# A two-layer decoder on one core: Gram products moved into the LoRA feed-forward, weights of the last stage loaded in one go, and a new row order in the first attention

## The reference

```
x = x + gqa(ln(x))            # 16 query heads, 4 key heads of 128, layer norm of q and k, rotation, causal
x = x + cross0(ln(x), ctx)    # 8 heads of 8 rows, no weights
x = x + lora_ffn(ln(x))       # W_base x + b, and one of 8 rank-16 experts chosen by a router
x = x + mqa(ln(x))            # 16 heads of 16, one key head
x = x + cross1(ln(x), ctx)    # 16 heads of 128, rms norm of q and k over all 2,048 columns
x = x + quantised_ffn(ln(x))  # int8-like rounding of rows and weights
```

## Time and profile before

| what | value |
|---|---|
| median of 3 runs | 3075.42 us (3070.69 to 3077.81) |
| profiled execution, its own time | 3078.19 us |
| span in the profile, first to last instruction | 3076.4 us |
| mean granted TensorE clock | 0.958 of full speed |
| busy: PE / DVE / ACT / POOL | 86 / 66 / 51 / 46% |

### The profile page before, as it was taken

The page is one execution under the profiler, slowest core; times in us unless marked ns, Lnnn a source line. Parts: engine busy times, 40 slices in busy tenths (PEclk is TensorE's granted clock), DMA queues, the critical chain, the costliest instruction groups (busy, mean ns, idle before and its releaser), DMA issues. The chain is left out here.

```text
span 3076.4 us, 86672 instructions
## 1 busy us (share of the span) xinstructions
PE 2646.2 (86%) x33275; PEld 1934.0 (63%) x33291; DVE 2017.7 (66%) x3674; ACT 1573.7 (51%) x2950; POOL 1405.2 (46%) x1522
## 2 busy tenths in 40 slices
PE   3888888888876888886779989999999999999576
PEld 2677777777751222222468867888888888888333
DVE  5888888888866788884878862343434343433697
ACT  3565555556544677772134433444444444444587
POOL 4888888888852223322434421222222222222487
PEclk9999999999996899997989989999999999999899
DMA  3000000000002232320011110000000000000000
GB/s 125 2 0 0 0 0 0 0 0 0 0 1 86 83 94 86 91 82 11 0 39 31 34 52 31 7 4 4 5 3 5 3 5 3 5 32 1 4 24 27
DMA packets 94668, 75.60 MB, mean 25 GB/s; under 512 B 17520, under 2 KB 88560, under 8 KB 93424
## 3 DMA queue, kind: packets, MB, share of 16 engines
q1 hardware_dynamic: 94576, 74.35, 7.9%
HBM read 55.97 MB, written 17.04 MB: 24 GB/s over the span
## 5 line engine op out<-in xcount | busy, mean ns | idle before, releaser
L1394 DVE TENSOR_REDUCE x_mx<-x_ps 128x2 f16<-128x512 f32 x512 | 332.8, 683 | 57.2 <-PE x_ps L1458 54.3
L1363 ACT ACTIVATE x_e<-x_ps 128x512 f32<-128x512 f32 x512 | 292.2, 596 | 55.1 <-PE x_ps L1462 38.1
L361 POOL TENSOR_TENSOR x1s<-x1s,x1mx 128x1024 f32<-128x1024 f32 x32 | 60.8, 1900 | 519.0 <-DVE x1mx L357 519.0
L1458 PE MATMUL x_ps<-x_k,x_q 32*128 32x256 f16 x1024 | 199.4, 292 | 80.9 <-ACT x_e L1363 48.0
L1722 ACT ACTIVATE x_q<-x_ps,x_q_bias,x_q_scale 128x128 f32<-128x128 f32 x512 | 185.7, 467 | 159.7 <-PE x_ps L105 159.7
L1458 PEld LDWEIGHTS x_ps<-x_k,x_q 32*128 32x128 f16 x1024 | 58.1, 93 | 269.4 <-DVE x_mx L1394 130.4
L431 ACT CAST x1oh<-x_ps 128x1024 f16<-128x1024 f32 x64 | 64.7, 1012 | 313.0 <-PE x_ps L423 313.0
L103 PE MATMUL a_ps<-ln_xha,a_wq 128*128 128x128 f16 x1024 | 180.3, 222 | 51.2 <-ACT a0v L678 44.0
L627 POOL TENSOR_TENSOR a_w<-a_qsw,a_tab 128x512 f32<-128x512 f32 x128 | 176.6, 1380 | 57.3 <-ACT a_qsw L688 56.0
L1462 PE MATMUL x_ps<-x_q,x_k 32*128 32x256 f16 x1024 | 201.0, 293 | 1.7 <-ACT x_e L1363 1.4
L280 DVE TENSOR_TENSOR ln_xlx<-x_ps,ln_xhx 128x256 f16<-128x256 f32 x32 | 13.6, 424 | 281.6 <-ACT x_xt L1714 281.6
(11 more groups left out here) (369 smaller groups left out, 9144.1 us busy)
## 6 DMA issues: line engine op xcount, KB each, us to landing
x_q<-x_q_rows SPq DMA_DIRECT2D x32, 256.0 KB, 2.8
x_k<-x_k_rows SPq DMA_DIRECT2D x32, 256.0 KB, 3.1
a_stage<-in_x_w SPq DMA_DIRECT2D x32, 256.0 KB, 2.6
x_vt<-in_ctx_v SPq DMA_DIRECT2D x32, 144.0 KB, 2.3
stage<-in_x_wt SPq DMA_DIRECT2D x4, 1028.0 KB, 6.4
x_all<-in_x SPq DMA_DIRECT2D x8, 512.0 KB, 10.0
x_cf<-in_ctx SPq DMA_DIRECT2D x32, 128.0 KB, 2.1
x_q_rows<-x_xhl SPq DMA_DIRECT2D x32, 128.0 KB, 1.7
```

The costliest lines, as they stand in the source:

```text
L1363: act.activation(e[:, u % ES].rearrange("p c n -> p (c n)"), s2_ps(u), ACT.Exp, scale=XT ** -0.5).then_inc(e_ready, 1)
L1394: dve.reduce_max(mx[:, p % 2, c:c + 2], s1_ps(u), AX).then_inc(mx_ready, 1)
L1458: return pe.matmul(s1_ps(u)[:, c], q[r, p % 4, g, c * P:(c + 1) * P], k[r, p % 4, g], start=True, stop=True)
```

## The change

1. The 32 weight products leave the head of `attention_cross`. `ffn_lora` makes one of them in every tile, between the projections of t+1 and `transpose_h` of t. Its weights arrive one head at a time (129 KB) into four buffers `wt`, loaded by SyncE. Both results of a half (16 heads) share bank 7, which a matmul with a zero operand opens; after tile 16 and after the last tile ScalarE and VectorE split them (`gram_high`, `gram_low`) into `gh`, `gl`, `g2`, which now live in tensors around both functions. `ht_ps` moves from bank 7 to the unused columns of the banks of `a_ps`. The new helper `over_halves` unrolls four tiles at the start, eight in the middle and four at the end.
2. In `attention_cross` SyncE loads the quantised ffn's weights right behind the first two context tiles, since `stage` has no other use.
3. In `attention_gqa` the order changes on three engines: TensorE makes the bias scores first in a step. VectorE takes `vq` ahead of the raw keys, sums the raw keys only before the maximum, takes query group 0 behind the denominator, normalisation and the low part of the output ahead of it, and the next rows' low part ahead of query group 3 and of the residual. ScalarE makes the swapped copy of group 0 before its squares, and the second high part of the output before the exponential. A query rotation now also waits for the squares.

```diff
+def over_halves(eng, head, step):
+    mid = TILES // 2
+    head()
+    for t in range(4):
+        step(t, t, True, 0)
...
 # attention_gqa, scalar: the copies are split off from square()
+            def swap_query(t, g):
+                act.wait_ge(q_ready, 4 * t + g + 1)
...
                 if has_next:
+                    swap_query(t + 1, 0)
                     square(t + 1, 0)
-                if has_next:
                     square(t + 1, 1)
-                at_.exponential(act, t)
-                if has_next:
-                    value(t + 1, 1 - p)
+                    swap_query(t + 1, 1)
                 if before:
                     at_.high(act, t - 1, 1, not has_next)
+                at_.exponential(act, t)
+                if has_next:
+                    value(t + 1, 1 - p)
 # attention_gqa, vector
-                if has_next:
-                    keys_raw(t + 1, 1 - p)
                 dve.wait_ge(var_ready, t + 1)
                 dve.tensor_scalar(vq[:, :], var_ps, ...)
                 if has_next:
-                    keys_summed(t + 1, 1 - p)
+                    keys_raw(t + 1, 1 - p)
+                    keys_summed(t + 1)
...
+                if has_next:
+                    keys_joined(t + 1, 1 - p)
                 at_.take_max(dve)
                 if has_next:
-                    rotate_query(t + 1, 0)
                     keys_scaled(t + 1, 1 - p)
                     rotate_query(t + 1, 1)
-                    add_swapped(t + 1, 0)
-                at_.denominator(dve, ch, t)
+                if further(t):
+                    ln.normalise(dve, t + 2, p)
                 if before:
                     at_.low(dve, t - 1, 1, not has_next)
-                if further(t):
-                    ln.normalise(dve, t + 2, p)
-                if has_next:
+                at_.denominator(dve, ch, t)
+                if has_next:
+                    rotate_query(t + 1, 0)
+                    add_swapped(t + 1, 0)
                     rotate_query(t + 1, 2)
                     add_swapped(t + 1, 1)
+                if further(t):
+                    ln.low(dve, t + 2, p)
+                if has_next:
                     rotate_query(t + 1, 3)
                 if before:
                     at_.add(dve, t - 1)
-                if further(t):
-                    ln.low(dve, t + 2, p)
 # attention_gqa, tensor
+                bias_scores(t, p)
                 if has_next:
                     keys(t + 1, 1 - p)
...
                 query_sums(t)
-                bias_scores(t, p)
 # ffn_lora, sync
+            def step(t, p, has_next):
+                wait_used(sp, wt_used, t, 4)
+                sp.dma_start(wt[:, p, :], dram_tile(d["x1_wt"], t)).then_inc(wt_in[p], 16)
+            over_tiles(sp, lambda: None, step, 4)
 # ffn_lora, scalar, after tile 16 and after the last
+            def gram_high(j):
+                act.wait_ge(wt_used, TILES // 2 * (j + 1))
+                for i, (src, twice) in enumerate(blocks):
+                    last = act.activation(gh[:, j, i], src, ACT.Copy, scale=twice * GRAM_SCALE)
+                last.then_inc(gh_ready, 1)
 # ffn_lora, vector, after tile 16 and after the last
+            def gram_low(j):
+                dve.wait_ge(gh_ready, j + 1)
+                for i, (src, twice) in enumerate(blocks):
+                    dve.scalar_tensor_tensor(gl[:, j, i], src, twice * GRAM_SCALE, gh[:, j, i], ALU.mult, ALU.subtract)
+                ...
 # ffn_lora, tensor
+            def weight_product(h, slot, start=False, stop=False):
+                pe.wait_ge(wt_in[slot], (h - slot) * 4 + 16)
+                w = wt[:, slot, :]
+                if start:
+                    pe.matmul(ps[:, 7, 0:GRAM + P + 1], zero[:, 0:P], zero[:, :], start=True, stop=False)
+                pe.matmul(g_high, w[:, 0:P], w, start=False, stop=False)
+                pe.matmul(g_low, w[:, P:2 * P], w[:, P:GRAM], start=False, stop=stop).then_inc(wt_used, 1)
...
+                if half == 0:
+                    weight_product(t, p, static and t == 0, static and t == TILES // 2 - 1)
+                elif static and t == TILES // 2 + 1:
+                    pe.wait_ge(gl_ready, 1)
+                    weight_product(t - 1, 0, True, False)
+                elif not (static and t == TILES // 2):
+                    weight_product(t - 1, (p - 1) % 4)
                 transpose_h(t, p)
...
 # attention_cross, sync
-            n = 2 * HEADS // GRAM_PIECES * GRAM
-            for i in range(GRAM_PIECES):
...
+            sp.dma_start(stage[:, 0:F1_COLS], d["f1_gu"]).then_inc(f1_in, 16)
+            sp.dma_start(stage[:, F1_COLS:], d["f1_down"]).then_inc(f1_in, 16)
...
-            sp.wait_ge(wt_used, GRAM_PIECES)
-            sp.dma_start(stage[:, 0:F1_COLS], d["f1_gu"]).then_inc(f1_in, 16)
-            sp.dma_start(stage[:, F1_COLS:], d["f1_down"]).then_inc(f1_in, 16)
 # attention_cross, scalar, vector and tensor heads: the splits, weight_products() and its wait go
-                weight_products()
-                pe.wait_ge(gl_ready, 2)
                 gram(0, 0)
```

148 lines of the change are left out of this document (78 added, 70 removed).

## The result

| | median us | runs | ratio to before, 95% interval |
|---|---|---|---|
| before | 3074.76 | 3070.69 to 3077.81, 4 | 1 |
| changed kernel | 3040.3 | 3037.72 to 3062.84, 4 | 0.9899 [0.9855, 0.9943] |
| changed kernel, timed again | 3049.14 | 3040.48 to 3054.78, 4 | 0.9921 [0.9894, 0.9948] |

A forecast was written before the change was run, and what follows sets the result against it. It took VectorE's chain to close the gqa step and TensorE alone to fill cross1's head; -37 (gqa), -23 (head) and +6 (LoRA ffn) gave -54, so 3021 us, own range 3003 to 3034, stated range 2985 to 3050.

The forecast's parts named there:

- 3039: Rival in gqa: the raw keys' sum waits for GpSimd's whole instruction (1.84 us), step gains only 0.60; chance 0.09.
- 3041: Rival in the LoRA ffn: the moved product is paid in full, +26 us there; chance 0.09.
- 3049: Rival in gqa: GpSimd closes the cycle, its late low squares leaving only 0.3 us gain a step; chance 0.14.
- From the keys to the scaled scores: Gqa step on VectorE: without the raw keys' sum, the scaled scores start right behind GpSimd's power, -0.49 us.
- From there to the low part of the rows: Gqa step on VectorE: denominator wait gone -0.57, low part earlier -1.38, raw keys' sum added +1.25 us.
- TensorE and GpSimd keep up: Gqa step: VectorE stays last with 1.0 us to spare; GpSimd's last low squares are the tight place.
- TensorE's bound: Rival in gqa: fewer port meetings, step shrinks by 2.2 us to what TensorE allows, 2990 us; chance 0.17.
- Gqa in all: Gqa stage: 31 steps, each 1.19 us shorter, -37 us, with ends of -55 and -31.
- Cross1's head: Start of the second cross attention: 32 weight products and their splits go, -23 us.
- The LoRA ffn: LoRA ffn: the product fits into TensorE's wait for routed rows; +6 us together, ends +3 and +26.
- Cross1's body: Second cross attention from 1862 us on: full of TensorE and not touched, so no term.
- The weights' loads at once: Quantised ffn's weights arriving at cross1's start: costs or gains nothing, since needed only hundreds of us later.

The follow-up runs named there:

- `join_back`: Changed kernel with VectorE's sum of the raw keys moved back ahead of the scaled scores; 3014.49 us, ratio 0.9805.
- `bias_back`: Changed kernel with TensorE's bias scores moved back behind the query sums; 3051.5 us, ratio 0.9928.
- `gqa_only`: Kernel before with only the new orders of gqa, without the move of the Gram products; 3053.29 us, ratio 0.9937.
- `gram_f1_late`: Kernel before with the Gram move, gqa as before, the first quantised projection's weights loaded behind the context loop again; 3066.24 us, ratio 0.9961.
- `rkd_quarter`: Changed kernel with GpSimd's spread of the key factors cut to a quarter from the second tile on (output differs); 3041.38 us, ratio 0.9892.
- `best_flat`: Changed kernel with the raw keys' sum back ahead of the scaled scores, TensorE's LoRA ffn loops written out, VectorE's query rotations reordered; 2999.1 us, ratio 0.9748.
- `join_rot2`: `join_back` with both VectorE query rotations ahead of the first `add_swapped`, the rows' low part ahead of the second; 3015.24 us, ratio 0.9801.

## Why the prediction was right and where not

The time of 3040 to 3049 is in the stated range of 2985 to 3050, 19 to 28 us above the forecast and outside its own range of 3003 to 3034. The direction and most terms were right; that the time is in the range is owed to its width, which was made for the rivals. The time alone would fit three of them (3039, 3041 and 3049), and the rows speak against each: the sum of the raw keys took 1.18 and not 1.84 us, the product lies in the wait, and GpSimd's squares hold nothing up. By its steps:

- **From the keys to the scaled scores**: forecast 7.78 us, measured 460.95 - 453.20 = 7.75. Right in size, wrong in reason. The text gave -0.49 to the sum of the raw keys leaving this stretch. `join_back` has the sum there and starts the scaled scores 0.15 behind the power; `bias_back` has it away, and starts them 0.62 behind. What had made them late was the chain ahead of the sum: in the kernel before, VectorE waited 1.50 us for TensorE's key sums (L750 above), which stood behind the bias scores. With the bias scores first and the raw keys behind `vq`, that wait is gone and the sum has room. With the bias scores back (`bias_back`) 0.38 us of it return.
- **From there to the low part of the rows**: forecast 17.49 - 0.57 - 1.38 + 1.25 = 16.79, measured 17.40. The wait ahead of the denominator did go, the low part does stand ahead of the last group, and the sum of the raw keys took 1.18 where 1.25 was taken. The missing 0.6 is in operations priced at no change: L843 +0.45 (1.82 for 1.37), L786 +0.45 (1.90 for 1.45), query group 0 +0.12 (0.72 for 0.60 to the next start), with -0.38 for the normalised rows (0.77 for 1.15). This is the step that failed: the text priced meetings with GpSimd only for the instruction that was moved, not for those that now stand elsewhere against GpSimd. The rival that the sum would wait for GpSimd's whole instruction did not come at its place; it nearly came at L843 and L786, which start 0.29 us into the spread of the key factors and 0.55 us into the subtraction of the maximum. The step read for 17.49 was also the shorter of two that alternate in the kernel before, 17.49 and 17.67 us.
- **TensorE and GpSimd keep up**: right. TensorE's bias scores fill the wait; neither GpSimd's late squares nor TensorE's bound shows: in the usual step `vq` starts 4.50 us behind the keys (457.70 - 453.20; 4.58 before).
- **Gqa in all**: 31 x -1.19 = -37 forecast; -0.68 in an undisturbed step, and two steps of 27.5 in the profiled execution, leave 17 us there (by the starts of `vq`). The ends of the stage gain too: its last residual starts 21.1 us earlier in the changed kernel, 22.1 in `gqa_only`, which measured -23 on the whole kernel.
- **Cross1's head**: -23 forecast, -24.2 to -24.8 measured.
- **The LoRA ffn**: +6 forecast, +6.2 to +7.4 measured (+3.4 to +3.8 from its first residual to its last, the rest at its ends). The product costs 0.65 and lies in the wait.
- **Cross1's body** was "not touched". Its instructions weren't, and it lost 9 to 12 us because they lie elsewhere in the program: a term the text didn't have. It takes about half, or more, of what the move of the Gram products gave (24.4 less 6.5). This is the second step that failed, a term that the text put at nothing.
- **The weights' loads at once**: nothing, shown by `gram_f1_late`.

The terms as measured in the changed kernel: 21 to 23 of gqa, 24.8 of the head, less 7 and less 9, are 30 to 32 us, and its times show 24 to 34.

## What to carry to other kernels

An operation of VectorE that reads two operands in SBUF beside a busy GpSimd has no fixed price: lay GpSimd's instructions beside it in the new order and price every such meeting, the neighbours' too, and put additions into time in which VectorE waits for a power or a matmul anyway. Before an addition is moved, ask which wait held what comes behind it; the instruction that stands in between need not be to blame. When code is added ahead of a long loop, look at the packets of the instruction queue: a loop near the size of what TensorE keeps can be fetched again in each iteration, and moving it to another place against the pieces can give the time back.

## What of the hardware was not expected

- The meeting of VectorE and GpSimd is exact: remaining time of GpSimd's instruction, plus the own time, less 0.13 us, to within 0.02 for the single additions that meet GpSimd between 200 and 800 us (93 in the kernel before, 118 in the changed one, 102 in `join_back`). The Trainium skill, "SBUF — State Buffer", section "SBUF: two separate sides", has it as an exclusive lock with a wait for the whole instruction; the trace agrees and adds the size. One instruction doesn't fit: beside the power on 16 columns, 2.90 us long, the sum of the raw keys takes 0.68 or 0.69 us, as if alone. Why is not shown.
- TensorE's loop of 6.92 pieces: 8 packets more in each iteration, by its place alone, and 0.1 to 1.1 us (every second tile takes 30.7 to 31.8 us instead of 30.66).
- Some gqa steps of the new order take 27.2 to 27.9 us among steps of 25.1 to 26.3: two and three in the two profiles of the changed kernel, two in `gqa_only`, one in `bias_back` and in `rkd_quarter` each, none in the kernel before, in `join_back` or in `best_flat`. In the changed kernel, the end of such a step, behind one row of the same place in the step ahead of it (columns of the earlier trace rows):

```profile
139.38:141.38 2.00, 0.56 (x6) 0.25 (x3) 2.00 (x3) 1.09 (x2) 2.00 (x2) 1.00 0.00 0
165.00:167.00 2.00, 0.64 (x6) 0.32 (x4) 2.00 (x3) 1.09 (x2) 2.00 (x2) 1.00 0.00 0
167.00:169.00 2.00, 1.66 (x6) 0.75 (x7) 1.98 (x4) 0.37 (x1) 2.00 (x3) 0.89 0.00 0
169.00:171.00 2.00, 2.00 (x22) 2.00 (x20) 2.00 (x3) 0.00 (x0) 2.00 (x2) 0.50 0.00 0
```

TensorE is busy 0.6 of 2 us in both, since it waits for VectorE's rotation; in one the granted clock stays at 1.00, in the other it falls to 0.50, which is 1.2 GHz, for some 3 us behind that wait. `join_rot2` and `best_flat`, which take the wait away, and `join_back`, in which it is 0.73 us, have no such step. But neither has the kernel before, with waits of 1.68 and 1.34 us in a step. Why the clock falls in one step and not in the next stays open.
